# A graph-network kernel: the feed-forward's addition and the residual follow the next block's weighing

## What is computed

```python
for l in range(2):
    xn = layernorm(h)
    q, k, v = xn @ wq[l] + bq[l], xn @ wk[l] + bk[l], xn @ wv[l] + bv[l]
    scores = einsum("ehd,ehd->eh", q[dst], k[src]) * scale      # also each node with itself
    attn = softmax over the edges of one dst
    h = h + segment_sum(attn * v[src], dst) @ wo[l] + bo[l]
    h = h + gelu(layernorm(h) @ w1[l] + b1[l]) @ w2[l] + b2[l]
# layer 2: the keys are K[src] + 0.2 * rel_w[type]; out = agg @ Wo + bo, residual, layernorm
```

## Time and profile before

| | us |
|---|---|
| median of 3 runs (lowest to highest) | 5655.94 (5652.53 to 5657.53) |
| the profiled execution, its span | 5652.02, 5650.4 |
| PE, DVE, ACT, POOL busy (share of the span) | 3852.2 (68%), 3863.6 (68%), 1896.3 (34%), 3129.7 (55%) |
| mean granted TensorE clock | 0.803 of 2.4 GHz |

### The profile page before, as it was taken

The page is one execution under the profiler, slowest core; times in us unless marked ns, Lnnn a source line. Parts: engine busy times, 40 slices in busy tenths (PEclk is TensorE's granted clock), DMA queues, the critical chain, the costliest instruction groups (busy, mean ns, idle before and its releaser), DMA issues. The chain is left out here.

```text
span 5650.4 us, 101635 instructions
## 1 busy us (share of the span) xinstructions
PE 3852.2 (68%) x17126; PEld 2788.6 (49%) x17127; DVE 3863.6 (68%) x6685; ACT 1896.3 (34%) x4023; POOL 3129.7 (55%) x3068
## 2 busy tenths in 40 slices
PE   2057664688887877746878778777746666666665
PEld 2023332466665665534656656555534455455444
DVE  9633333787776666637877766666469989888876
ACT  5023331233333333322333343333422333333333
POOL 0422224777666655426777655554267777666643
PEclk9987776788888988877989888888866766766666
DMA  4022224676666555436666665554256665555542
GB/s 180 7 62 93 94 94 123 188 216 205 191 184 189 172 166 155 136 106 187 212 213 195 190 192 171 162 162 146 81 145 180 184 178 167 163 163 154 144 131 84
DMA packets 361805, 870.95 MB, mean 154 GB/s; under 512 B 142032, under 2 KB 154813, under 8 KB 361748
## 3 DMA queue, kind: packets, MB, share of 16 engines
q0 software_dynamic: 243088, 718.69, 43.2%
q1 hardware_dynamic: 111604, 119.56, 6.8%
q10 hardware_dynamic: 7056, 32.12, 1.4%
HBM read 791.89 MB, written 149.65 MB: 167 GB/s over the span
## 5 line engine op out<-in xcount | busy, mean ns | idle before, releaser
L1039 POOL DMA_INDIRECT kv<-kv_dram,idx x2616 | 2699.7, 1032 | 1598.8 <-issue 751.2
L1506 PE MATMUL ps_acc<-kv,ident 128*128 x5232 | 1499.1, 457 | 328.9 <-DVE kv L1179 327.7
L1506 PEld LDWEIGHTS ps_acc<-kv,ident 128*128 128x128 f32 x5232 | 1218.6, 236 | 635.2 <-issue 412.1
L1101 DVE TENSOR_TENSOR kv<-kv,ps_q 128x1024 f32 x654 | 785.0, 1213 | 177.1 <-issue 103.7
L1106 DVE TENSOR_REDUCE sc<-kv 128x32 f32 (+2 forms) x654 | 785.5, 1211 | 17.5 <-DVE kv L1101 13.1
L1179 DVE TENSOR_TENSOR kv<-kv,ps_q x654 | 753.6, 1216 | 20.7 <-issue 8.2
L1500 PE MATMUL ps_acc<-acc_scaled,ident 128*128 128x256 f32 x306 | 149.2, 581 | 567.1 <-DVE zrun L1171 567.1
L1557 PE MATMUL ps_big<-xnaT,w_ffn 128*128 128x128 f32 x3136 | 389.4, 284 | 142.5 <-ACT xnaT L1407 142.5
L1557 PEld LDWEIGHTS ps_big<-xnaT,w_ffn 128*128 128x128 f32 x3136 | 372.1, 198 | 164.4 <-ACT xnaT L1407 83.0
L1407 ACT ACTIVATE xnaT<-ps_t,ln 128x128 f32<-128x128 f32 x196 | 79.0, 453 | 1068.5 <-PE ps_t L585 898.7
L1500 PEld LDWEIGHTS ps_acc<-acc_scaled,ident 128*128 128x128 f32 x306 | 61.5, 251 | 620.6 <-DVE zrun L1171 620.6
(11 more groups left out here) (206 smaller groups left out, 5024.8 us busy)
## 6 DMA issues: line engine op xcount, KB each, us to landing
rec_in<-rec_dram SPq DMA_DIRECT2D x147, 512.0 KB, 5.1
rec_dram<-rec_out POOLq DMA_DIRECT2D x98, 512.0 KB, 3.4
kv<-kv_dram,idx POOLq DMA_INDIRECT x2616, 3.7
rec_dram<-rec_in ACTq DMA_DIRECT2D x49, 640.0 KB, 3.0
windows<-kv SPq DMA_DIRECT2D x46, 408.0 KB, 2.6
rec_in<-rec_dram SPq DMA_DIRECT2D x49, 128.0 KB
w_ffn<-in_L_gnn_w SPq DMA_DIRECT2D x4, 1024.0 KB, 6.4
meta<-slot_meta SPq DMA_DIRECT2D x153, 24.0 KB, 2.6
```

The source lines that it names most:

```text
L1039: pool.indirect_dma_start(kv[:, u * W + slot, :], None, kv_dram[l], bass.IndirectOffsetOnAxis(ap=idx[:, u, slot:slot + 1], axis=0), bounds ...
L1101: nc.vector.tensor_tensor(at, at, q, ALU.mult).then_inc(s["mul"], 1)
L1506: mm = nc.tensor.matmul(ps_acc[:, 0:D], ident[:], at[:, :, slot, :].rearrange("p a d -> p (a d)"), start=False, stop=False, skip_group_che ...
```

## The change

Nothing is computed otherwise. On DVE `second(b - 2)` and `residual(b - 1)` go from ahead of the maxima and of `rescale` to the end of the iteration, behind `weigh`; `scales1` and `scales2` go from behind `rescale` to the head of the next iteration, behind `start`, so that they are one block further back. On ACT `record(b - 3)` goes ahead of the square roots, and `normed1` ahead of `normed2`. On PE `feed_out` is cut in two halves of four products, with `project_sums` between them; q of the next layer is written into the free half of the bank of `ps_t`, so that it need not wait for `second`; and the wait for `recq` stands once at the head of the iteration. The iterations before and after each hardware loop are 2 in layer 2 where they were 3.

```diff
--- before.py
+++ after.py
@@ -207,7 +207,8 @@
         eps_col = sb("eps_col", [P, 1])
 
 
-        ps_t = pb("ps_t", [P, 512])[:, 0:D].rearrange("p (c n) -> p c n", c=KD)
+        ps_t_q = pb("ps_t_q", [P, 512])
+        ps_t = ps_t_q[:, 0:D].rearrange("p (c n) -> p c n", c=KD)
         ps_t2_w = pb("ps_t2_w", [P, 512])
         ps_t2 = ps_t2_w[:, 0:D].rearrange("p (c n) -> p c n", c=KD)
         ps_w = pb("ps_w", [P, 512])
@@ -923,13 +924,13 @@
                 last, chunks_before, earlier, rounds_before = counts
                 return (round_number(rounds_before + earlier), chunks_before + earlier * CPS, last)
 
-            def iterate(eng, iteration, peeled=DEPTH, whole=NB - 1 if typed else NB):
+            def iterate(eng, iteration, peeled=2 if typed else DEPTH, whole=NB - 1 if typed else NB):
 
                 for b in range(peeled):
                     iteration(b)
                 with eng.Fori(peeled, whole) as b:
                     iteration(b)
-                for b in range(whole, NB + DEPTH):
+                for b in range(whole, NB + peeled):
                     iteration(b)
 
             def last_block(b):
@@ -1271,10 +1272,16 @@
                         def second_part():
                             if exists(b - 2):
                                 second(b - 2)
+                        def earlier_scales():
+                            if exists(b - 2):
+                                scales1(b - 2)
+                            if exists(b - 3) and not typed:
+                                scales2(b - 3)
                         if exists(b):
                             counts = blocks.next(b)
                             k, chunk0, filled = last_round(counts)
                             start(b)
+                            earlier_scales()
 
                             def finish_last():
                                 if exists(b - 1):
@@ -1304,23 +1311,17 @@
                                 with dve.If(earlier == 0):
                                     finish_last()
                             scores(b, k, chunk0, filled, finish_late if late else lambda: None)
-                            second_part()
                             maxima(last, k, chunk0, filled)
+                            rescale(last, b, k)
+                            weight_sums(b, k)
+                            weigh(k, chunk0, filled)
                         else:
+                            earlier_scales()
                             if exists(b - 1):
                                 finish(b - 1, dve.snap(blocks.rounds, min_val=1))
-                            second_part()
+                        second_part()
                         if exists(b - 1):
                             residual(b - 1)
-                        if exists(b):
-                            rescale(last, b, k)
-                        if exists(b - 2) and not typed:
-                            scales2(b - 2)
-                        if exists(b - 1):
-                            scales1(b - 1)
-                        if exists(b):
-                            weight_sums(b, k)
-                            weigh(k, chunk0, filled)
 
                     extras = dve.alloc_register(f"l{l}_extras")
                     dve.reg_mov(extras, 0)
@@ -1447,7 +1448,7 @@
                         to = rec_out[:, one(b % OUT_RING), :]
                         act.wait_ge(s["qkv"], b + 1)
                         nc.scalar.copy(flat(to[:, :, 0:2 * D]), ps_kv)
-                        nc.scalar.copy(flat(to[:, :, 2 * D:3 * D]), ps_w[:, 0:D]).then_inc(s["recq"], 1)
+                        nc.scalar.copy(flat(to[:, :, 2 * D:3 * D]), ps_t_q[:, D:2 * D]).then_inc(s["recq"], 1)
 
                     def iteration(b):
                         if exists(b - 2) and not typed:
@@ -1472,18 +1473,18 @@
                             if typed and not last_block(b):
                                 relation_rows(next_round(k))
                             exp_round(k, None if last_block(b) else b + 1)
+                        if exists(b - 3) and not typed:
+                            record(b - 3)
                         if exists(b - 2) and not typed:
                             act.wait_ge(s["var2"], b - 1)
                             deviation(1, s["sd2"])
                         if exists(b - 1):
                             act.wait_ge(s["var1"], b)
                             deviation(0, s["sd1"])
+                        if exists(b - 1):
+                            normed1(b - 1)
                         if exists(b - 2) and not typed:
                             normed2(b - 2)
-                        if exists(b - 1):
-                            normed1(b - 1)
-                        if exists(b - 3) and not typed:
-                            record(b - 3)
                         if exists(b):
                             free_unused(k, filled)
 
@@ -1559,16 +1560,15 @@
                             if f % 4 == 3:
                                 mm.then_inc(s["f1"], 1)
 
-                    def feed_out(b):
+                    def feed_out(b, half):
                         to = ps_w[:, D:2 * D]
-                        if not isinstance(b, int) or b >= 2:
-                            pe.wait_ge(s["recq"], b - 1)
-                            settle(pe)
-                        bias(to, B_2 + l * D)
-                        for f in range(KF):
+                        if half == 0:
+                            bias(to, B_2 + l * D)
+                        for f in range(half * KF // 2, (half + 1) * KF // 2):
                             pe.wait_ge(s["g"], b * KF + f + 1)
                             mm = nc.tensor.matmul(to, gT[:, f, :], w_2[:, f, :], start=False, stop=(f == KF - 1))
-                        mm.then_inc(s["f2"], 1)
+                        if half == 1:
+                            mm.then_inc(s["f2"], 1)
 
                     def turn_normed(b):
                         pe.wait_ge(s["xn2"], b + 1)
@@ -1582,12 +1582,12 @@
                         project_kv(l + 1, xnbT)
 
                     def next_q(b):
-                        if not isinstance(b, int) or b + 1 < NB:
-                            pe.wait_ge(s["second"], 2 * b + 3)
+                        project_q(ps_t_q[:, D:2 * D], l + 1, xnbT).then_inc(s["qkv"], 1)
+
+                    def iteration(b):
+                        if exists(b - 4) and not typed:
+                            pe.wait_ge(s["recq"], b - 3)
                             settle(pe)
-                        project_q(ps_w[:, 0:D], l + 1, xnbT).then_inc(s["qkv"], 1)
-
-                    def iteration(b):
                         if exists(b - 2) and not typed:
                             turn_hidden(b - 2)
                         if exists(b - 3) and not typed:
@@ -1597,12 +1597,14 @@
                         if exists(b - 1):
                             turn_sums(b - 1)
                         if exists(b - 2) and not typed:
-                            feed_out(b - 2)
-                        if exists(b - 3) and not typed:
-                            pe.wait_ge(s["xTs2"], b - 2)
-                            settle(pe)
+                            feed_out(b - 2, 0)
                         if exists(b - 1):
+                            if exists(b - 3) and not typed:
+                                pe.wait_ge(s["xTs2"], b - 2)
+                                settle(pe)
                             project_sums(b - 1)
+                        if exists(b - 2) and not typed:
+                            feed_out(b - 2, 1)
                         if exists(b - 3) and not typed:
                             next_kv(b - 3)
                         if exists(b):
```

## The result

| | before | changed |
|---|---|---|
| median, us (lowest to highest of 4 runs each) | 5654.23 (5650.90 to 5657.53) | 5782.28 (5777.14 to 5784.12) |
| ratio, 95% interval | | 1.0225 [1.0207, 1.0243] |
| profiled execution, us; mean granted clock | 5652.02; 0.803 | 5784.12; 0.798 |

A forecast was written before the change was run, and what follows sets the result against it. No engine was full; in layers 0 and 1 DVE, PE and ACT took turns in one round trip. 225 + 86 + 8 - 100 = 219 us off 5652.0 gave 5433, as a median 5437 us, range 5355 to 5560.

The forecast's parts named there:

- Part 1: Layers 0 and 1: `second` and `residual` behind `weigh` drop waits of 267.8 us, moved scales 38 us, in 66 blocks.
- Part 2: Layers 0 and 1: VectorE's wait for the exponentials lies bare, 1.22 us a block, 81 us lost in 66 blocks.
- Part 3: Layers 0 and 1: POOL and PE stay under DVE's loop; blocks of 3 chunks gain 86 us, of 2 some 8.
- Part 4: Layer 2, with no feed-forward to wait for: `second` and `residual` lie bare behind `weigh`, 100 us lost (0 to 160).
- The halves of `feed_out`: On PE: cutting `feed_out` in two halves moves nothing by itself, since ACT copies `aggT` just as half is done.
- A: Rival, chance 0.16: PE is late next, 2 us above DVE's loop in 66 blocks, half the gain, 5569 us.
- B: Rival, chance 0.10: layer 2 loses 20 us in place of 100, as the relation rows come forward, 5357 us.
- D: Rival, chance 0.05: the last feed-forward product is still late at `weigh`'s end, half of the wait left, 5618 us.
- C: Rival, chance 0.03: TensorE's clock at its lower level for two thirds of the loop, slower than before, 5750 us.

The follow-up runs named there:

- the best kernel: Changed kernel with layer 2 in the old order; layers 0 and 1 with `second`, `residual` ahead of `weigh`'s last two chunks and an early one-column exponential: 5307.51 us.

## Why the prediction was wrong, by its own steps

**The step that failed** is in parts 1 and 4 alike: "The instructions stay as they are, and so does their own cost." The sum took VectorE's idle time between two blocks over from the kernel before, where it was nothing. It never named what hid the head, and what that would cost with the cover gone. The term was 0 and measured 340.9 us (147 blocks, 2.3 us each). The profiled execution was forecast at 5433 and took 5784, 351 more; the missing term is 97% of it. That the two meet so closely is in part luck: the 24 us between the layers had no term either, and some smaller misses take them back. With the gap the stages come out as follows (us a block, forecast + gap against measured): layer 0 28.2 + 2.3 against 30.8, 25.1 + 2.5 against 27.6, 23.0 + 2.4 against 24.9; layer 2 with 4 chunks 31.5 + 2.3 against 33.5.

**Part 1, the waits that go: right.** The f2 waits of the earlier trace rows are gone, the square root waits of those stages too. The sum for a block of 5 chunks gives 28.3 us and not 28.2 (30.7 - 3.0 - 0.6 + 1.2), which changes nothing.

**Part 2, the answer bare: right**, 2.38 us in each block of 5 and 4 chunks where 2.37 was taken. That the code of the exponentials isn't touched was a reason to keep the number, and it held.

**Part 3, who is late next: mostly right.** GpSimd's pace of 28.0 is the 28.1 of the best kernel; in the changed one VectorE is slower than that, with its gap. So "no idle time on POOL at 5 chunks" did not come: it waits there some 3 us a block for VectorE (39.3 us, 13 times, in 1200 to 1600). PE was not late at 5 and 4 chunks: VectorE waits there for nothing of PE, and for ACT only the bare 2.38. In layer 1 the loops are 31.9, 29.3 and 27.3 us where the working of part 1 gives 29.2 and 25.9 and part 3 took 24.0, so that with gaps of 2.3, 3.2 and 2.4 there 0.4, 0.2 and 0.9 stay. At 5 and 4 chunks TensorE's clock is not the reason, since nobody waits for it; VectorE's own busy time is 0.2 to 0.3 us a block longer than before (24.4 for 24.1 and 20.9 for 20.7), which part 1 had kept as it was. At 3 chunks the exponentials are late, as part 3 had feared for PE and ACT: VectorE waits for them 3.1 us in layer 0 and 4.6 in layer 1. That was not taken apart.

**Part 4, layer 2 pays: the mechanism right, the gap missing.** 100 us were forecast and 188 measured; the gap is 105 of them, and 83 are left for what part 4 counted. The bare `second` and `residual` of the earlier trace rows are there, the wait for the exponentials is 4.7 us where 4.8 was forecast, and the gap comes on top. A 4-chunk block shows all three:

```profile
4987.98 0.18 DVE L571 BATCH_NORM_AGGREGATE mv<-bns 128x2 f32<-128x6 f32 x1
4990.44 0.07 DVE L1194 MEMSET mrun<- 128x8 f32 x1 [2.27 <-issue]
...
5007.87 0.26 DVE L1160 TENSOR_TENSOR sm<-sm,mrun 128x100 f32<-128x100 f32 x1
5012.49 0.42 DVE L1168 TENSOR_TENSOR acc_scaled<-acc,ps_q 128x256 f32<-128x256 f32 x1 [4.36 <-ACT ps_q L1362]
```

**The halves of `feed_out`, "nothing by themselves": true in company, not alone.** In VectorE's old order PE's and ACT's new orders together cost 1.9 to 3.3 us a block in layers 0 and 1; the halves were not run without the rest.

**The rivals.** A, B and D did not come. C, the only one on the slower side, gave the sign with the wrong mechanism: its lower level did not come up more often where it was to decide: in the 5-chunk stage of layer 0 the clock rose from 0.89 to 0.94, and the mean over the kernel fell from 0.803 to 0.798 only. The rival that came was on no list, since every rival was looked for among waits and busy engines; the sequencer's work is neither.

**Left open.** Why the two loads take 0.8 us each in the 4-chunk blocks of layer 1. There they fall into a stretch in which all DMA engines are busy with the gathers of blocks and a record (352 GB/s on average in 3503.9 to 3507.5), while in 1572.5 to 1575 nearly nothing was moved and they took 0.30. Busy DMA engines alone do not explain it: VectorE made 148 of its loads in the changed kernel while the DMA engines were busy for 80% or more of the time (from 0.5 us before the load to its end); their median is 0.32 us, though 32 of the 34 loads of over 0.6 us are among them. No run varied it.

## What to carry to other kernels

Before a step is moved to the end or the head of a loop's iteration, look at the sequencer's rows there (branch, value loads, asserts), add them up, and name the instructions ahead of them that wait for nothing: those are the cover. If the moved step waits on itself, put it ahead of the last such instructions and not behind them; here that alone was worth 180 us. And a wait that looks small next to the largest one may be the cheaper to remove: the table load, taken out of line in the kernel before, with its order as it was, gave 153 us.

## What the runs showed of the hardware

- A value load on VectorE's sequencer takes 0.30 us, and with its registers and assert 0.64 us of VectorE's time on average where nothing covers it (four loads, 373 us in 147 blocks); in one stage 0.82 us at the median for the load alone.
- VectorE's sequencer runs ahead over products that wait for nothing: it came to the loop's head 3.4 us before the last of five products of 1.15 us ended. Behind a chain in which each step waits for the one before it had no lead (the head from 1572.55 on, the last step from 1572.53 to 1572.71).
- A step of an iteration can be free at one place and cost its full length at another: the loop's head took 0 us behind five products, 0.3 behind two and 2.3 behind `residual` (0.95 there without its two loads).
- In these kernels the table load came behind the wait that stands ahead of the function (1702.23, after the subtraction from 1701.70 on); an exponential of one column ahead of the wait drew it forward, and the answer fell from 2.38 to 1.1 us.
- The same 40 matmuls of TensorE's sums took 8.87 us at the whole clock, 11.02 at 0.80 and 11.7 at 0.76. The idle time just ahead does not tell which: with 0.59 us both 8.87 and 11.5 were seen.
